# Five full expert tiles taken ahead of the last batch's routing, in both MoE layers of a four-layer hybrid kernel

## The chip, the cores and the metric

The kernel runs on one core of one Trainium2 chip. The metric is device time in microseconds (us) for the whole program, median of three runs. Engines are named as in the profile: PE is TensorE, DVE is VectorE, ACT is ScalarE, POOL is GpSimd, SP is SyncE, which here only starts transfers.

## What is computed

Four residual layers over x of shape 4 x 256 x 256 (1024 tokens, in eight tiles of 128): attention A, MoE, attention B, MoE, each on a layernorm of x. All in float32.

```
x = x + attn_a(layernorm(x))     # 16 heads; rotary parts; causal
x = x + ffn(layernorm(x))
x = x + attn_b(layernorm(x))     # 32 heads of 8, 8 KV heads; causal
x = x + ffn(layernorm(x))        # the same weights as the first ffn

def ffn(x):                      # E = 8 experts, I = 688, top 2
    logits = xf @ router_w.T
    top_vals, top_idx = top_k(logits, 2)
    top_w = softmax(top_vals)
    combine = sum(one_hot(top_idx, E) * top_w[..., None], axis=1)
    for e in range(E):
        h = silu(xf @ Wg[e].T) * (xf @ Wu[e].T)
        out = out + combine[:, e:e+1] * (h @ Wd[e].T)
```

## The kernel before

Layers are numbered 0 (attention A), 1 (MoE), 2 (attention B), 3 (MoE). Every engine has its own program, written out in order at the end of the file; semaphores tie them together.

**Attention** goes batch by batch (4 batches, b = 0 to 3), in groups of four heads: 4 groups in layer 0, 8 in layer 2. For a group, PE makes scores, then shifted scores (`shifted_tensor`), ACT their exponentials, PE the product with V (`pv_tensor`, L515 and L519), DVE copies it out (`pv_vector`), PE transposes it (`out_t_tensor`, L532), DVE divides (`divide_vector`). After the last group of a batch: `all_t_tensor` (L542), `out_scalar`, `project_tensor` (L555), `add_vector`.

**Routing** of batch b-1 is woven into attention of batch b: layernorm (`norm_tensor`, L351), logits (L1093), the two largest (`largest_vector`), then `rank_tensor` (L1104), which counts with bf16 matmuls how many earlier tokens chose the same expert, and `slots_vector` (ends at L1136), which turns ranks into addresses. POOL then writes the tokens into a table `slots_in` in HBM, ordered by expert (four indirect transfers L1207), and their numbers into `row_of_slot` (four more, L1210). The last batch has nothing to be woven into: `route_last_*` does it after attention, and `tiles_vector` (L1144 to L1161) then makes the list of expert tiles.

**Expert tiles.** 2048 routed rows over 8 experts need at most 23 tiles of 128 rows. For each: SP loads the rows (L1219), PE transposes them (L1252), `tile_up` makes gate and up products (L1265, 16 matmul records in the trace), ACT the SiLU, DVE the product (L1326), PE transposes the hidden rows (`tile_hidden`, L1276), DVE and ACT copy them, `tile_down` (L1287, 12 records) multiplies by the down weights, ACT copies out and POOL scatters the result (L1241) and loads the next tile's row numbers (L1232, L1233). PE reads the tile's expert number from the list with a register load (`expert_of`, L1256). The loop is software-pipelined: hidden(i-1), transpose(i+1), up(i), down(i-1).

**Where the weights lie.** All gate/up weights live in `wgu` (eight experts of 1376 KB), all down weights in `R1` (5504 KB). Attention A uses the same room before: queries and keys of even batches (0, 2) lie in `R1`, those of odd batches (1, 3) in the places of experts 5 to 7 of `wgu`; smaller buffers lie in experts 3 and 4. So SP loads experts 0 to 2 early, the down weights after batch 2's last shifted scores (in two transfers, L1500 and L1501), then experts 3, 5, 6, 7, 4, of which 5 to 7 wait for batch 3's last shifted scores. In layer 2 the last batch's queries and keys lie in `R2`, where the expert tiles keep their rows too.

Of the kernel before, what the change touches and what calls it, by code (L numbers as in the profile page):

```python
# [17 lines left out]
P = 128  # L18
# [26 lines left out]

SLOTS = E * T + (SLOTS_T - ROUTED // P) * P
# [4 lines left out]
def shape_constants():  # L51

    def bf16(x):
# [24 lines left out]
        np.arange(24, dtype=np.float32) * P,  # L78
    ]).astype(np.float32)
# [8 lines left out]
def build_hybrid(nc, dr, out):  # L88

    ctx = ExitStack()  # L90
    with ctx:
# [29 lines left out]
        def room(o, n):  # L121
            return wgu[:, o:o + n]

        ODD = 5 * KD * GU
        stacks = [(R1[0:RA, 0:HA * S], R1[0:RA, HA * S:2 * HA * S]),
                  (room(ODD, HA * S)[0:RA, :], room(ODD + HA * S, HA * S)[0:RA, :])]
# [11 lines left out]
        assert o <= ODD  # L138
# [44 lines left out]
        small = wb[:, o:o + 200]; o += 200  # L183
# [15 lines left out]
        o = 0  # L199
        cmp = XN[:, 1024 + o:1024 + o + 72].rearrange("p (e j) -> p e j", j=E); o += 72  # L200
        ntl = XN[:, 1024 + o:1024 + o + E]; o += E
        base = XN[:, 1024 + o:1024 + o + E + 1]; o += E + 1
        ecm = XN[0:1, 1024 + o:1024 + o + 24 * E].rearrange("p (i e) -> p i e", e=E); o += 24 * E
        ecb = XN[0:1, 1024 + o:1024 + o + 24 * E].rearrange("p (i e) -> p i e", e=E); o += 24 * E
        eidf = XN[0:1, 1024 + o:1024 + o + 24]; o += 24
        first = XN[0:1, 1024 + o:1024 + o + 24]; o += 24
        rowf = XN[0:1, 1024 + o:1024 + o + 24]; o += 24
        eid = XN[0:1, 1024 + o:1024 + o + 24].bitcast(I32); o += 24
        row = XN[0:1, 1024 + o:1024 + o + 24].bitcast(I32); o += 24
        rows = XN[:, 1024 + o:1024 + o + 2].bitcast(I32); o += 2  # L210
        assert o <= 1024
# [16 lines left out]
        xn_b = R2[:, 5632:6144].rearrange("p (t d) -> p t d", t=2)  # L228

# [80 lines left out]
        def normed_rows(l, b):  # L310


            if l in (0, 2):
                return xn[:, 2 * b:2 * b + 2, :]
            return xn[:, 0:2, :] if b == B - 1 else xn_a if l == 1 else xn_b
# [4 lines left out]
        def normed_vector(l, b):  # L320
# [4 lines left out]
            if l in FF:  # L325
                later(v, s["transposed"], b)
                if 0 < b < B - 1:
                    v.wait_ge(FF[l][f"scatter{(b - 1) % 2}"], 64 * ((b - 1) // 2 + 1))
# [216 lines left out]

        def project_tensor(l, b):
# [6 lines left out]
            for t in range(2):  # L553
                for kk in range(KD):
                    last = nc.tensor.matmul(BK[6][:, t * D:(t + 1) * D], oT[:, kk, t * P:(t + 1) * P], wo[:, kk, :],  # L555
# [3 lines left out]
        def add_vector(l, b):  # L559
# [3 lines left out]
            nc.vector.tensor_tensor(xb, xb, BK[6][:, :].rearrange("p (q d) -> p q d", q=2), ALU.add).then_inc(s["added"], 1)  # L563
# [69 lines left out]
        def attend_a_tensor(b):  # L633
            max_tensor(0, b)
            nc.tensor.wait_ge(AT[0]["max_e"], b + 1)
            for g in range(GA):
# [7 lines left out]
                if g >= 1:  # L644
                    pv_tensor(0, b, g - 1)
                if g == 1 and b > 0:
                    logits_tensor(1, b - 1)
                if g == 2 and b > 0:
                    nc.tensor.wait_ge(FF[1]["copied"], b)
# [4 lines left out]
        def end_a_tensor(b, step):  # L654
            if step == 0:
                pv_tensor(0, b, GA - 1)
                if b > 0:
                    nc.tensor.wait_ge(AT[0]["divided"], b * GA + GA - 2)
                    rank_tensor(1, b - 1)
            if step == 1:  # L660
                if b > 0:
                    nc.tensor.wait_ge(FF[1]["slot"], b)
# [4 lines left out]
        def end_a_vector(b, step):  # L667
            if step == 0:
                pv_vector(0, b, GA - 1)
                if b > 0:  # L670
                    slots_vector(1, b - 1)
# [14 lines left out]
        def attend_a_vector(b):  # L686
            for g in range(GA - 1):
                pv_vector(0, b, g)
                if g == 0 and b > 0:
                    logits_vector(1, b - 1)  # L690
                if g >= 1:
                    divide_vector(0, b, g - 1)
                if g == 2 and b > 0:
                    largest_vector(1, b - 1)
# [24 lines left out]
        def attend_b_tensor():  # L719
# [3 lines left out]
            for n in range(RUN + 3):  # L723
# [6 lines left out]
                if g >= 5 and b > 0:  # L730
                    nc.tensor.wait_ge(AT[2]["divided"], n - 2)
                if g == 5 and b > 0:
                    norm_tensor(3, b - 1)
                if g == 6 and b > 0:
# [972 lines left out]
```

## Time and profile before

| what | value |
|---|---|
| median of 3 runs | 941.76 us (940.12 to 944.01) |
| the profiled execution | 940.44 us, span 938.5 us |
| PE busy | 793.6 us, 85% of the span |
| DVE, ACT, POOL busy | 358.8, 246.9, 223.5 us |
| L1265, up products, PE | 223.2 us |
| L1287, down products, PE | 127.0 us |

The span is the first to the last instruction of the program. The page's row of granted clock is in tenths of full speed; PE is granted either full speed (2.4 GHz) or half (1.2 GHz), and a slice with 7 in it holds both. PE's row of busy tenths (40 equal slices) falls to 6 and 4 in slices 12 and 13 and to 8 and 2 in slices 30 and 31: these are the two places between an attention and its MoE, and the places of the change. The 7, 3, 3, 7 of slices 21 to 24 is the end of the first MoE and the start of attention B, which the change doesn't touch.

### The profile page before, as it was taken

How to read it: one execution, taken by the hardware profiler on the slowest of the kernel's cores; microseconds unless marked ns; L12 is line 12 of the kernel's file. 1: busy time of each engine (PE TensorE's matmuls, PEld its weight loads, DVE VectorE, ACT ScalarE, POOL GpSimd, SP SyncE). 2: the span in 40 equal slices, each digit the busy share in tenths (PEclk: the TensorE clock that was granted, in tenths of full speed). 3: DMA queues.
4: the chain of work that ended last, by engine and by line, in shares of the span. 5: the costliest groups of instructions: out<-in, count | busy, mean ns of one | idle time of the engine just before them, and what ended most of it. 6: DMA issues, size and time to landing. Idle time of an engine off the chain costs nothing.

```text
span 938.5 us, 14815 instructions
## 1 busy us (share of the span) xinstructions
PE 793.6 (85%) x5008; PEld 605.5 (65%) x5009; DVE 358.8 (38%) x860; ACT 246.9 (26%) x493; POOL 223.5 (24%) x260
## 2 busy tenths in 40 slices
PE   1989899999964999999973379999982999999990
PEld 1767677777743777777752347777762777777770
DVE  8444253653432212212235576576443222222112
ACT  1102104123322222222213204545451222222221
POOL 8441022340233112221123400012324111222212
PEclk9999899999985999999995779999995999999995
DMA  6963904125953061000203451120402001110004
GB/s 186 404 145 123 321 27 113 35 58 118 272 218 113 29 218 48 34 32 25 66 23 90 130 142 33 41 61 31 155 24 67 21 31 34 34 34 34 28 18 140
DMA packets 47472, 88.09 MB, mean 94 GB/s; under 512 B 8667, under 2 KB 36699, under 8 KB 45307
## 3 DMA queue, kind: packets, MB, share of 16 engines
q1 hardware_dynamic: 35887, 54.49, 20.7%
q0 software_dynamic: 7568, 30.97, 9.1%
q10 hardware_dynamic: 3968, 1.97, 0.8%
q8 instruction: 32, 0.52, 0.2%
q14 instruction: 17, 0.14, 0.1%
HBM read 52.27 MB, written 35.13 MB: 93 GB/s over the span
## 4 chain that ended last, share of the span: by engine, by line
PE 80%; DVE 8%; DMA 5%; issue 2%; ACT 1%; POOL 1%; SPq 1%; ACTq 0%; POOLq 0%; DVEq 0%
PE bank L1265 23%; PE bank L1287 13%; PE bank L860 8%; PE bank L486 4%; PE bank L441 4%; PE bank L1276 3%; PE bank L497 3%; PE bank L515 3%; PE bank L431 2%; PE bank L484 2%; PE bank L555 2%; PE bank L532 2%; DMA PTR<-rows_out 2%; DVE stat L308 2%; PE bank L1252 1%
## 5 line engine op out<-in xcount | busy, mean ns | idle before, releaser
L1265 PE MATMUL bank<-wgu,R 128*128 x736 | 223.2, 457 | 0.0
L1265 PEld LDWEIGHTS bank<-wgu,R 128*128 128x128 f32 x736 | 138.1, 193 | 64.9 <-issue 2.1
L1287 PE MATMUL bank<-R 112*128 (+1 forms) x552 | 127.0, 379 | 1.3 <-DVE R L1329 1.3
L1326 DVE TENSOR_TENSOR R<-R,bank 128x344 f32<-128x344 f32 x92 | 47.2, 513 | 194.7 <-PE bank L1265 194.7
L1287 PEld LDWEIGHTS bank<-R 112*128 112x128 f32 (+1 forms) x552 | 104.7, 190 | 22.6 <-issue 1.8
L625 ACT ACTIVATE PTR<-bank 128x512 f32<-128x512 f32 x144 | 83.5, 597 | 86.8 <-PE bank L486 71.5
L1241 POOL DMA_INDIRECT rows_out<-R,XN x46 | 46.5, 1011 | 177.4 <-ACT R L1317 162.8
L1329 DVE COPY R<-bank 112x512 f32<-112x512 f32 x46 | 31.8, 691 | 112.4 <-PE bank L1276 112.4
L1303 ACT ACTIVATE R<-bank 128x344 f32<-128x344 f32 x92 | 42.0, 457 | 118.7 <-PE bank L1265 118.7
L574 DVE TENSOR_REDUCE XN<-bank 128x2 f32<-128x512 f32 x96 | 63.1, 684 | 9.3 <-PE bank L441 9.3
L1317 ACT ACTIVATE R<-bank 128x256 f32<-128x256 f32 x46 | 17.7, 384 | 152.6 <-PE bank L1287 152.6
L1233 POOL DMA_DIRECT2D XN<-row_of_slot x46 | 25.7, 558 | 133.4 <-issue 130.8
L570 DVE TENSOR_REDUCE XN<-bank 128x4 f32<-128x512 f32 x48 | 33.1, 689 | 45.6 <-PE bank L431 45.0
L484 PE MATMUL bank<-XN,sel_sb 96*128 96x256 bf16 x192 | 49.7, 276 | 0.0
L595 DVE COPY XN<-bank 128x256 f32<-128x256 f32 x48 | 20.2, 420 | 76.2 <-PE bank L519 75.9
L903 POOL TENSOR_TENSOR R<-wgu 128x256 f32<-128x256 f32 x32 | 23.2, 724 | 108.0 <-DVE wgu L875 102.8
L351 PE MATMUL bank<-ident_sb,XN 128*128 128x128 f32 x40 | 9.3, 381 | 45.9 <-DVE XN L331 45.9
L1207 POOL DMA_INDIRECT slots_in<-R,stat x12 | 11.6, 970 | 144.6 <-DVE stat L1136 141.9
L860 PE MATMUL bank<-xnT,R 128*128 128x256 f32 (+2 forms) x176 | 41.5, 392 | 2.3 <-DVE wgu L875 1.5
L860 PE MATMUL bank<-wgu,R 96*128 96x256 f32 (+1 forms) x176 | 40.7, 384 | 0.8 <-issue 0.8
L860 PEld LDWEIGHTS bank<-xnT,R 128*128 128x128 f32 (+2 forms) x176 | 31.9, 186 | 11.1 <-issue 5.1
L1276 PE MATMUL bank<-ident_sb,R 128*112 128x128 f32 (+1 forms) x276 | 37.8, 273 | 1.4 <-DVE R L1326 1.4
(159 smaller groups left out, 1250.8 us busy)
## 6 DMA issues: line engine op xcount, KB each, us to landing
wgu<-in_wgu SPq DMA_DIRECT2D x10, 1376.0 KB, 9.8
slots_in<-PTR POOLq DMA_DIRECT2D x1, 9088.0 KB, 26.7
row_of_slot<-in_unused POOLq DMA_DIRECT2D x2, 4544.0 KB, 17.3
R<-slots_in SPq DMA_DIRECT2D x46, 128.0 KB, 2.0
R<-R SPq DMA_DIRECT2D x32, 128.0 KB, 2.4
wgu<-R SPq DMA_DIRECT2D x32, 128.0 KB, 2.4
PTR<-rows_out SPq DMA_DIRECT2D x16, 256.0 KB, 3.2
R<-in_wd SPq DMA_DIRECT2D x1, 3584.0 KB, 17.3
```

The lines of the kernel that those rows point to most:

```text
L441: last = nc.tensor.matmul(bank[1 + i][:, j * S:(j + 1) * S], q(h)[:, P:S], k(h)[:, :], start=False, stop=j == 1, skip_group_check=True)
L484: nc.tensor.matmul(bank[i][:, j * S:(j + 1) * S], sel[:, h:h + 1].broadcast_to([PARTS * 32, P]), nT[:, :], start=False, stop=False, skip_g ...
L486: last = nc.tensor.matmul(bank[i][:, j * S:(j + 1) * S], k(h)[:, 0:P], q(h)[:, :], start=False, stop=j == 1, skip_group_check=True)
L574: nc.vector.tensor_reduce(nmax[:, 1, 4 * g + 2 * i:4 * g + 2 * i + 2], bank[1 + i][:, :].rearrange("p (n s) -> p n s", n=2), AX, ALU.max, ...
L625: nc.scalar.activation(PT[:, g % 2, i, :], banks(l, g, True)[i][:, :], ACT.Exp, scale=scale).then_inc(s["exps"], 1)
L860: last = nc.tensor.matmul(dst, w, r, start=kk in (0, None), stop=kk in (1, None))
L1241: g.indirect_dma_start(y_d[:, :], bass.IndirectOffsetOnAxis(ap=rows[:, p:p + 1], axis=0), yo[:, p, :], None).then_inc(s[f"ys{p}"], 16)
L1265: last = nc.tensor.matmul(BK[2 * half + gu][:, 0:IH], xsT[:, p, kk, :], wgu[:, bass.ds(e * (KD * GU) + (kk * GU + gu * I + half * IH), IH) ...
L1276: last = nc.tensor.transpose(BK[4 + c // 4][0:CH[c], (c % 4) * P:(c % 4 + 1) * P], hh[:, CO[c]:CO[c] + CH[c]], ident[:, :])
L1287: last = nc.tensor.matmul(BK[7][:, 0:D], hT[0:CH[c], p, c, :], wd[0:CH[c], bass.ds(e * (6 * D) + c * D, D)], start=c == 0, stop=c == 5)
L1303: a.activation(sg[:, half * IH:(half + 1) * IH], BK[2 * half][:, 0:IH], ACT.Silu).then_inc(s["silu"], 1)
L1326: v.tensor_tensor(hh[:, half * IH:(half + 1) * IH], sg[:, half * IH:(half + 1) * IH], BK[2 * half + 1][:, 0:IH], ALU.mult).then_inc(s["hid ...
```

## The change

Batches 0 to 2 send 1536 rows to 8 experts. However they fall, at least `FULL_T` = 5 tiles of 128 rows are full by then. The changed kernel lists five such tiles once batch 2 is routed, and runs them while batch 3 is routed; the other 18 tiles come from a second list (`REST_T`). The number of tiles stays 23.

- `tiles_vector` is called twice: by `full_tiles_vector` (17 short DVE instructions, during attention of the last batch) and for the rest (15, after the last batch's slots).
- `finish_tensor`, `finish_vector`, `finish_scalar` replace `route_last_*` and the first steps of `experts_*`: an order written out by hand that weaves the last batch's transposes, projection, layernorm, logits and rank into tiles 0 to 3.
- In attention, logits and rank of the batch before come one step earlier, and rank is moved from the end of a batch (layer 0) or group 7 (layer 2) into the groups.
- The places are exchanged: even batches' queries and keys lie in experts 5 to 7, odd ones' in `R1`. So SP loads 5, 6, 7, 3, 4 after batch 2, and the down weights are loaded after batch 3's last shifted scores, on POOL's queue (`load_down_gpsimd`).
- Batch 2's normed rows of layer 1 get a buffer of their own (`xn_c`). Down products of tiles 0 to 3 go to bank 5, since bank 7 serves the routing.

```diff
+BEFORE = (B - 1) * S * TOPK
+FULL_T = (BEFORE - E * (P - 1) + P - 1) // P
+REST_T = SLOTS_T - FULL_T
@@ attend_a_vector
-                pv_vector(0, b, g)
                 if g == 0 and b > 0:
                     logits_vector(1, b - 1)
+                    largest_vector(1, b - 1)
+                if g == 1 and b > 0:
+                    slots_vector(1, b - 1)
+                pv_vector(0, b, g)
+                if g == 1 and b == B - 1:
+                    full_tiles_vector(1)
@@ finish_tensor(l)
+            out_t_tensor(a, b, heads(a)[0] - 1)
+            nc.tensor.wait_ge(FF[l]["eid"], 1)
+            nc.tensor.wait_ge(s_wgu, 16 * (E if l == 1 else E + 2))
+            e = [expert_of(i) for i in range(FULL_T)]
+            tile_transpose(l, 0, 0, 0)
+            tile_transpose(l, 1, 0, 1)
+            tile_up(l, 0, 0, 0, e[0], [0])
+            all_t_tensor(a, b)
+            tile_up(l, 0, 0, 0, e[0], [1])
+            project_tensor(a, b)
+            hidden_and_next(0, 0, 0)
+            tile_up(l, 1, 0, 1, e[1])
+            norm_tensor(l, b)
+            nc.tensor.wait_ge(s_wd, 32)
+            tile_down(l, 0, 0, 0, e[0])
+            logits_tensor(l, b)
+            hidden_and_next(1, 0, 1)
+            tile_up(l, 2, 1, 0, e[2], [0])
+            rank_tensor(l, b)
+            tile_up(l, 2, 1, 0, e[2], [1])
+            tile_down(l, 1, 0, 1, e[1])
...
+            tile_down(l, 3, 1, 1, e[3])
+            nc.tensor.wait_ge(FF[l]["eid"], 2)
+            tile_transpose(l, 5, 2, 1)
+            nc.tensor.wait_ge(FF[l]["y_e"], FULL_T - 1)
@@ experts_gpsimd(l)
+            tile_gpsimd(l, 0, 0, 0)
+            tile_gpsimd(l, 1, 0, 1)
+            scatter_gpsimd(l, B - 1)
+            tile_gpsimd(l, 2, 1, 0)
+        def load_down_gpsimd():
+            nc.gpsimd.wait_ge(AT[0]["shifted"], B * 3 * GA)
...
+            nc.gpsimd.dma_start(wdv[0:CH[0], :, 0:4 * D], dr["wd4"].rearrange("e p m -> p e m")).then_inc(s_wd, 16)
+            nc.gpsimd.dma_start(wdv[0:CH[5], :, 4 * D:6 * D], dr["wd2"].rearrange("e p m -> p e m")).then_inc(s_wd, 16)
@@ experts_sync(l), before the first rows are loaded
+            if l == 3:
+                nc.sync.wait_ge(AT[2]["shifted"], B * 3 * GB)
```

The order on PE at the end of attention A, before the change. L1104 is rank, L532 the transposes of single groups, L542, L555, L351 and L1093 the last batch's, L1256 the register load, L1252 the first tiles' transposes.

```order
L519 MATMUL bank<-PTR,vaug 32x128 x4
L1104 MATMUL bank<-wb 128x8 x11
L532 MATMUL bank<-ident_sb,XN 128x128 x4
L542 MATMUL bank<-ident_sb,XN 128x128 x4
L555 MATMUL bank<-R,XN 128x256 x4
L351 MATMUL bank<-ident_sb,XN 128x128 x4
L1093 MATMUL bank<-wb,xnT 128x8 x4
L1104 MATMUL bank<-wb 128x8 x23
L1256 TENSOR_LOAD XN
L1256 ISA x2
L1252 MATMUL bank<-ident_sb,R 128x128 x4
```

The same place after it, from the same product with V (now L537). L1364 are tile transposes, L1377 up products, L560 is all_t, L576 the projection, L1390 hidden transposes, L369 the layernorm's.

```order
L537 MATMUL bank<-PTR,vaug 32x128 x4
L550 MATMUL bank<-ident_sb,XN 128x128 x4
L1368 TENSOR_LOAD XN
L1368 ISA x2
L1364 MATMUL bank<-ident_sb,R 128x128 x4
L1377 MATMUL bank<-wgu,R 128x344
L560 MATMUL bank<-ident_sb,XN 128x128 x4
L576 MATMUL bank<-R,XN 128x256 x4
L1390 MATMUL bank<-ident_sb,R 112x128 x4
L369 MATMUL bank<-ident_sb,XN 128x128 x4
L1404 MATMUL bank<-R 128x256
L1113 MATMUL bank<-wb,xnT 128x8 x4
```

Rows that only repeat are left out here: the register load stands five times, the up product eight times for tile 0 (four on each side of all_t) and eight for tile 1 between L1390 and L369. Two tiles' worth of up products now stand between the last product with V and the last batch's layernorm.

POOL's order in layer 1, after the change. L1319 and L1322 are the scatters of a batch, L1589 and L1590 the down weights, L1345 loads row numbers, L1353 scatters a tile's result.

```order
L1319 DMA slots_in<-R,stat 9088x256 x4
L1322 DMA row_of_slot<-wb,stat 9088x128 x4
L1589 DMA R<-in_wd 112x8x1024
L1590 DMA R<-in_wd 120x8x512
L1344 TENSOR_LOAD XN
L1345 DMA XN<-row_of_slot 128x1
L1353 DMA rows_out<-R,XN 11136x256
L1319 DMA slots_in<-XN,stat 9088x256 x4
```

Before, batch 3's scatter followed batch 2's at once, and no weights were on this queue. Now the down weights stand behind batch 2's eight scatters, and batch 3's scatter (`slots_in<-XN`) behind the results of tiles 0 and 1 (left out: the second row load and the second tile's rows, which repeat).

## Rows read from the trace of the kernel before

**Rows 1.** Page, part 4: shares of the chain that ended last.
```profile
PE 80%; DVE 8%; DMA 5%; issue 2%; ACT 1%; POOL 1%; SPq 1%; ACTq 0%; POOLq 0%; DVEq 0%
```
**Rows 2.** PE's longest wait from 260 to 310 us: in total, times, longest.
```profile
PE bank L1252 <- DMA R<-slots_in: 9.9, 1, 9.9
```
**Rows 3.** PE's timeline around layer 1: start, us, what, idle time before it.
```profile
242.13 0.60 PE L542 MATMUL bank<-ident_sb,XN 128*128 128x128 f32 x4
243.42 1.99 PE L555 MATMUL bank<-R,XN 128*128 128x256 f32 x8 [0.69 <-ACT XN L630]
...
266.81 0.64 PE L515 MATMUL bank<-PTR,vaug 128*32 128x256 f32 x8 [0.27 <-DVE XN L595]
...
268.60 0.42 PE L1104 MATMUL bank<-wb 128*128 128x8 bf16 x11 [0.93 <-DVE wb L1125]
...
281.34 1.08 PE L351 MATMUL bank<-ident_sb,XN 128*128 128x128 f32 x4 [3.54 <-DVE XN L331]
...
297.42 0.66 PE L1252 MATMUL bank<-ident_sb,R 128*128 128x128 f32 x2 [9.85 <-DMA R<-slots_in]
...
299.09 5.95 PE L1265 MATMUL bank<-wgu,R 128*128 x16
...
313.87 0.82 PE L1276 MATMUL bank<-ident_sb,R 128*112 128x128 f32 x6
...
314.75 4.79 PE L1265 MATMUL bank<-wgu,R 128*128 x16
319.38 2.76 PE L1287 MATMUL bank<-R 112*128 x12
...
338.17 0.82 PE L1276 MATMUL bank<-ident_sb,R 128*112 128x128 f32 x6
```
**Rows 4.** PE's timeline around layer 3, same columns.
```profile
699.50 0.41 PE L532 MATMUL bank<-ident_sb,XN 128*128 128x128 f32 x2 [0.65 <-DVE XN L605]
...
723.31 0.66 PE L1252 MATMUL bank<-ident_sb,R 128*128 128x128 f32 x2 [9.77 <-DMA R<-slots_in]
...
764.44 0.82 PE L1276 MATMUL bank<-ident_sb,R 128*112 128x128 f32 x6
```
**Rows 5.** Stretches: engines' busy us and counts, granted clock, DMA share, GB/s.
```profile
270.00:275.00 5.00, 2.97 (x10) 1.87 (x11) 1.00 (x4) 1.46 (x2) 3.87 (x4) 0.57 1.01 419
...
300.00:305.00 5.00, 5.00 (x15) 2.79 (x14) 0.51 (x1) 1.94 (x3) 1.15 (x2) 0.86 0.10 27
```
**Rows 6.** Line L1256 from 270 to 340 us: duration ns min/median/max, first and last start.
```profile
L1256 PEldq FUSED_REGOPS  x14: 46/151/165, 292.2 to 335.5; - x14
L1256 PEldq TENSOR_LOAD <-XN x11: 298/302/483, 291.7 to 335.1; - x11
```
**Rows 7.** DVE's timeline, first and last instruction of the tile list in layer 1.
```profile
288.33 0.22 DVE L1144 TENSOR_TENSOR XN<-bank,wb 128x64 f32<-128x64 f32 x1
...
291.49 0.17 DVE L1161 CAST XN<-XN 1x24 int32<-1x24 f32 x1
```
**Rows 8.** POOL's timeline: batch 2's scatters, first and last; a tile's result and row load.
```profile
270.15 0.97 POOL L1207 DMA_INDIRECT slots_in<-wgu,stat  x1 [26.37 <-DVE stat L1136]
...
279.06 0.96 POOL L1210 DMA_INDIRECT row_of_slot<-wb,stat  x1 [0.30 <-issue]
...
741.54 1.01 POOL L1241 DMA_INDIRECT rows_out<-R,XN  x1 [11.35 <-ACT R L1317]
745.15 0.55 POOL L1233 DMA_DIRECT2D XN<-row_of_slot  x1 [2.61 <-issue]
```
**Rows 9.** DMA issues in layer 1: count, KB each, us from issue to landing.
```profile
R<-in_wd SPq DMA_DIRECT2D x1, 3584.0 KB, 17.3
R<-in_wd SPq DMA_DIRECT2D x1, 1920.0 KB, 28.2
...
slots_in<-XN,stat POOLq DMA_INDIRECT x1, 2.4
...
R<-slots_in SPq DMA_DIRECT2D x1, 128.0 KB, 2.1
```

More of the change, by code:

```diff
@@ L197, in build_hybrid, with passed @@
         assert o <= KD * (D + 2 * KVB * HDB), o
[L199 to L211, printed above, removed]
+        o = 1536
+        cmp = XN[0:1, o:o + 72].rearrange("p (e j) -> p e j", j=E); o += 72
+        ntl = XN[0:1, o:o + E]; o += E
+        base = XN[0:1, o:o + E + 1]; o += E + 1
+        jump = XN[0:1, o:o + E + 1]; o += E + 1
+        left = XN[0:1, o:o + E]; o += E
+        over = XN[0:1, o:o + E]; o += E
+        total = XN[0:1, o:o + E]; o += E
+        assert o <= 1664
+        o = 1672
+        eid = XN[0:1, o:o + 24].bitcast(I32); o += 24
+        row = XN[0:1, o:o + 24].bitcast(I32); o += 24
+        rows = XN[:, o:o + 2].bitcast(I32); o += 2
+        taken = XN[0:1, o:o + E]; o += E
+        eidf = XN[0:1, o:o + 24]; o += 24
+        rowf = XN[0:1, o:o + 24]; o += 24
+        def passed(n, at):
+            return [XN[0:1, at + k * n * (E + 1):at + (k + 1) * n * (E + 1)].rearrange("p (i e) -> p i e", e=E + 1)
+                    for k in range(2)]
+        early_lists, late_lists = passed(FULL_T, o), passed(REST_T, 1024)
+        assert o + 2 * FULL_T * (E + 1) <= 1896 and 1024 + 2 * REST_T * (E + 1) <= 1536
         FILLS = 8
@@ L722, in attend_b_tensor @@
             max_tensor(2, 0)
-            for n in range(RUN + 3):
+            for n in range(RUN + 1):
                 b, g = n // GB, n % GB
@@ L762, in attend_b_vector @@
             parts_vector(2, 0)
-            for n in range(RUN + 3):
+            for n in range(RUN + 1):
                 b, g = n // GB, n % GB
@@ new lines, in tiles_vector @@
+            if not first:
+                link(v.tensor_tensor(left, ntl, taken, ALU.subtract),
+                     v.tensor_tensor(jump[:, 0:E], jump[:, 0:E], taken, ALU.add))
+            link(v.tensor_tensor(cmp, (ntl if first else left)[:, None, :].broadcast_to([1, E + 1, E]),
+                                 small[0:1, 80:152].rearrange("p (e j) -> p e j", j=E), ALU.mult))
+            link(v.tensor_reduce(base, cmp, AX, ALU.add))
+            link(v.tensor_tensor(ecm, small[0:1, 152:152 + n, None].broadcast_to([1, n, E + 1]),
+                                 base[:, None, :].broadcast_to([1, n, E + 1]), ALU.is_ge))
@@ L1274, in tile_hidden @@
             later(nc.tensor, s["hte_s"], i)
-            for c in range(6):
+            for c in chunks:
+                if c == 4 and isinstance(i, int):
+                    later(nc.tensor, s["y_e"], i)
                 last = nc.tensor.transpose(BK[4 + c // 4][0:CH[c], (c % 4) * P:(c % 4 + 1) * P],
@@ L1555, in _ @@
             project_b_gpsimd()
-            for b in range(B):
+            for b in range(B - 1):
                 scatter_gpsimd(3, b)
@@ L1578, in _ @@
                 attend_a_vector(b)
-            for step in range(3):
+            for step in range(2):
                 end_a_vector(B - 1, step)
-            add_vector(0, B - 1)
-            route_last_vector(1)
+            finish_vector(1)
             experts_vector(1)
@@ L1643, in _ @@
                 attend_a_tensor(b)
-            for step in range(3):
+            for step in range(2):
                 end_a_tensor(B - 1, step)
-            all_t_tensor(0, B - 1)
-            project_tensor(0, B - 1)
-            route_last_tensor(1)
+            finish_tensor(1)
             experts_tensor(1)
```

333 lines of the change are left out of this document (194 added, 139 removed).

## The prediction, made before the changed kernel ran

> **What bounds the kernel now.** Read the shares of the last chain first: PE holds 80% of it, DMA 5% [rows 1]. So the kernel is bound by PE's work, and time can only be won where PE stands still. PE's waits next: in the stretch from 260 to 310 us it stood 9.9 us for the first expert rows [rows 2], and 3.54 us for the last batch's layernorm [rows 3]. The timeline then gives the whole hole. The last product with V starts at 266.81 and the first tile's transposes at 297.42, and only the last batch's short steps lie between [rows 3]. In layer 3 the same hole runs from the last group's transpose at 699.50 to 723.31 [rows 4]. Last, the granted clock: 0.57 in the stretch from 270 us, 0.86 in that from 300 us [rows 5], so PE fell to half speed in the hole and came back only after the first up products had run for a while (5.95 us against 4.79 us for the same sixteen later, 1.2 us lost) [rows 3]. Once it runs, PE has no gaps: a tile takes 8.10 us, from (338.17 - 313.87) / 3 [rows 3].
>
> I follow one mark through before and after, the start of the hidden transposes of tile 4: 338.17 in layer 1 and 764.44 in layer 3 [rows 3, 4]. Behind that mark the same 18 tiles follow, PE-bound in both kernels. The time won is how much earlier the mark comes, once for each layer.
>
> **1. The attention loops.** Logits and rank change places with products with V; the matmuls stay, but for six more small ones in the rank of batch 2. In group 2 PE now waits for the slots (five dependent DVE instructions, at the 0.25 us of those of the tile list [rows 7] some 1.2 us) behind one product with V (0.64 us and a shorter one [rows 3]), in place of a similar wait at the end of a batch. I cost batches 1 and 2 at nothing, 1 us either way. For the last batch in layer 1 the rank (0.42 us before [rows 3], 0.5 with its six more) and 0.6 us of that wait now lie ahead of the last product with V: it starts at 267.9 instead of 266.81 [rows 3]. It ends at 268.7. A group's transposes cost 0.41 us and 0.65 of wait for the division before them [rows 4]; of the two groups left, one wait is covered: 1.1 to 1.5 us, 269.8.
>
> The first tile list is 17 DVE instructions. The 13 of the old list took 3.3 us (288.33 to 291.66) [rows 7], so about 3.8 us. In layer 1 a group's float32 scores and product on PE hide them. In layer 3 a group's scores are bf16 and short, and the next copy of a product with V stands behind the list on DVE: PE waits between 0 and the whole 3.8 us, and I take 2, as about half of it finds cover in one group. The last transpose comes at 701.3 instead of 699.50 [rows 4].
>
> **2. Up to the first tile.** PE needs five expert numbers. One load is 0.30 us, with register work of 0.15 us behind it, the first 0.48 us [rows 6]: 2.6 us, and with the small gaps between them I take 3.1. Nothing else can run on PE meanwhile. The rows themselves are there in time: batch 2's scatter starts about 262.3 instead of 270.15 [rows 8], its fourth write lands 3.8 + 2.4 us later and the load of the rows takes 2.1 [rows 9], some 270.8. So the first tile's transposes start at 269.8 + 3.1 = 272.9 in layer 1 (before: 297.42 [rows 3]) and 701.3 + 3.1 = 704.4 in layer 3 (before: 723.31 [rows 4]).
>
> **3. From there to the wait for the down weights.** Transposes and up products of tile 0 at a half-speed start, as before: 299.09 + 5.95 - 297.42 = 7.6 us. Inserted: all_t 0.6 and projection 2.0 (at full speed [rows 3]). Hidden transposes and the next tile's: 314.75 - 313.87 = 0.9. Up products of tile 1: 319.38 - 314.75 = 4.6. Layernorm's transposes 0.5 (1.08 at half speed [rows 3]). Sum 16.2: PE is at the wait at 289.1 in layer 1 and at 720.6 in layer 3. ACT's table loads for square root and SiLU, and the layernorm on DVE, fit under these.
>
> **4. The down weights.** They are now asked for after batch 3's last shifted scores, and POOL first has to issue eight scatters of batch 2. Those took from 270.15 to 280.02, 9.9 us [rows 8]; from 262.3 they end at 272.2, and the weights are issued at about 272.8. How long the load takes is the largest unknown. Before, the pair took 28.2 us from issue to landing of the second [rows 9], with one batch's scatters (0.75 MB) among it, which I take off as 2 us: 26. The low bound is what all transfers together reached when gate/up weights were loaded, 419 GB/s [rows 5]: 5504 KB in 13.5 us. I take 26, since it is this same transfer with the same shapes: it lands at 298.8. PE stands for 9.7 us, falls to half speed again and loses another 1.2 us when it starts. In layer 3 the weights are there, and this term is nothing.
>
> The Trainium skill, page "DMA: Bandwidth & Descriptors", section "Anatomy of one DMA", gives 2.0 us plus the bytes at 436 GB/s for a transfer from GpSimd's queue; by it the pair would take about 15 us and land at 288, and PE would not wait. The row of before (17.3 us for the first alone) speaks against it. The same page, section "Latency and other measured facts", tells of copies that fall to about half the rate when rows lie a large power of two apart; that would keep this load slow on any queue, and no run here shows it yet.
>
> **5. From the wait to the mark.** Down 0, three steps of 8.10, logits 1.0, rank 0.4, tile 5's transposes and a short wait for a bank 0.5, less the transposes that step 3 doesn't have 0.2: 2.6 + 24.3 + 1.7 = 28.6 us. Layer 1: 298.8 + 28.6 + 1.2 = 328.6, that is 9.6 us earlier than 338.17. Layer 3: 720.6 + 28.6 = 749.2, 15.2 us earlier than 764.44.
>
> **6. The last batch's rows.** They are needed for tile 5. POOL scatters tiles 0 and 1 first: from the end of down 1 there are 0.8 us to POOL's start, 4.2 us for the result and the next row load (741.54 to 745.70 [rows 8]), then three scatter steps of 1.27, 2.4 to land, 0.8 for SP, 2.1 to load [rows 8, 9]: 14.2 us. PE needs 16.0 us from there to the transposes of tile 5. Hidden, with 1.8 us in hand; if that cover goes, each us over it is paid twice, once for each layer.
>
> **Sum.** 9.6 + 15.2 = 24.8 us. The profiled execution took 940.44 us, 1.3 under the median, so 915.6 against it; I predict 916.0.
>
> **Rivals.**
> A. The down weights come fast (any time from 14 to 17 us). Then PE doesn't wait in layer 1 and keeps its clock: 9.7 + 1.2 more, 905. For it: gate/up weights of a similar size did run at 419 GB/s [rows 5], and fewer other transfers run now. Against: 17.3 and 28.2 us for the same bytes [rows 9]. Anything between gives 905 to 916.
> B. Rows come late. The loads of tiles 2 and 3 run while the down weights fill all engines, and tile 5's rows hang on a chain with 1.8 us in hand. If POOL's writes land in 6 us instead of 2.4, PE waits 2 us twice; if tile 2's rows wait for the whole load, up 1 and the layernorm (5 us) come after it instead of under it. 919 to 926.
> C. The clock stays low. Between the tiles PE now does short steps with waits. If it ran at half speed from the first transposes to the mark, 45 us of work would take 90, in both layers 90 us more, against 25 won: about 1005, slower. It decides from about 25 us of extra time, that is if over a quarter of the stretch is at half speed. Against it: in the rows of before, full speed came back within 3 us of the first up products (1.2 us lost [rows 3]).
> D. The first tiles don't come early at all, because PE also waits for all eight gate/up weights and the list. The five loads begin where the down weights did, a whole batch of groups ahead. They are 6880 KB against 5504, so even at the slow rate of [rows 9] they take 35 us (28.2 x 1.25), and the first tile starts later than that. If they came only with the rest, all would be as before, 940.
>
> **How the numbers follow.** The forecast (911 to 919): 0.50. A and what lies between: 0.27. B: 0.17. C: 0.02. D and small gains: 0.04. The range of 903 to 924 holds A, the forecast and most of B. A measurement of this kernel can tell 0.5% (4.7 us) from no change. Faster by over that 0.96, within 0.02, slower 0.02.
>
> **What would show it.** In the profile after: PE's longest wait in layer 1 is that of the first down products for `R<-in_wd`, near 10 us (A: under 1). Time from issue to landing of the two: near 26 us. The first tile's transposes at about 273 and 704. Granted clock of 1.0 from there but for that wait. No wait of over 1 us at tile 5's transposes; if there is one, B. Hidden transposes of tile 4 at 329 and, in layer 3, 15 us earlier relative to the last product with V than the old one. The prediction is wrong if PE waits for anything else for over 3 us between the marks, or if batches 1 and 2 cost more than 1 us each in either attention.

## The result: 931.4 us, 11 us faster where 25 were forecast

The changed kernel took 931.37 us (median of 4 runs, 930.45 to 933.83) against 942.38 us for the kernel before: ratio 0.9895, 95% interval 0.9871 to 0.9919. The sign was right and the size was not: the time lies above the range of 903 to 924. The profiled execution has a span of 928.7 us, 9.8 under that of before; the ratio gives 9.9 us. A label such as x2 names a run of the section on the experiments.

The page's part 4 of the changed kernel (shares of the chain that ended last) answers to [rows 1]:

```profile
PE 74%; DMA 8%; DVE 8%; issue 6%; POOL 2%; ACT 1%; SPq 0%; ACTq 0%; POOLq 0%; DVEq 0%
```

DMA went from 5% to 8% because the load of the down weights, 27.32 us, now lies on the chain. The rise of "issue" from 2% to 6% is for the most part no stall of PE. The chain in order of time (start, us, what) shows where it lies; its 4.95 us have their like before the change (4.47):

```profile
103.59 4.95 issue
...
233.64 28.39 issue
...
332.34 2.12 issue
...
752.23 2.10 issue
```

From the weights the chain goes back to POOL, which issued them behind batch 2's scatters and had stood idle for 28.6 us before the first of these, until the slots came at 262.26. PE worked in that stretch, so a good part of its fall from 80% to 74% is this detour too. Only the two pieces of 2.1 us are new stalls of PE's sequencer on this chain. PE's timeline around layer 1 (start, us, what, idle time before it) answers to [rows 3]:

```profile
269.79 0.41 PE L550 MATMUL bank<-ident_sb,XN 128*128 128x128 f32 x2 [0.72 <-DVE XN L627]
...
273.54 0.69 PE L1364 MATMUL bank<-ident_sb,R 128*128 128x128 f32 x2 [3.34 <-issue]
...
300.48 5.28 PE L1404 MATMUL bank<-R 112*128 x12 [10.82 <-DMA R<-in_wd]
...
312.60 2.76 PE L1404 MATMUL bank<-R 112*128 x12
...
331.75 0.39 PE L1364 MATMUL bank<-ident_sb,R 128*128 128x128 f32 x2
334.46 0.84 PE L1390 MATMUL bank<-ident_sb,R 128*112 128x128 f32 x6 [2.33 <-issue]
```

The first tile starts 24 us earlier than at 297.42 [rows 3]. Then PE stands 10.8 us for the down weights, runs tile 0's down product in 5.28 us instead of 2.76, and stands 2.3 us more right at the mark, which comes at 334.46: 3.7 us earlier than 338.17 [rows 3], where 9.6 were forecast. The same in layer 3, beside [rows 4]:

```profile
706.92 0.69 PE L1364 MATMUL bank<-ident_sb,R 128*128 128x128 f32 x2 [3.16 <-DMA R<-slots_in]
...
722.84 2.76 PE L1404 MATMUL bank<-R 112*128 x12
...
754.32 0.84 PE L1390 MATMUL bank<-ident_sb,R 128*112 128x128 f32 x6 [2.31 <-issue]
```

That mark is 10.1 us earlier than 764.44 [rows 4], so layer 3 itself gave 6.4 where 15.2 were forecast. The weights' landing (DMA issues, KB each, us from issue to landing) stands beside [rows 9], and the stretches (engines' busy us and counts, granted clock, DMA share, GB/s) beside [rows 5]:

```profile
R<-in_wd POOLq DMA_DIRECT2D x1, 3584.0 KB, 18.5
R<-in_wd POOLq DMA_DIRECT2D x1, 1920.0 KB, 27.3
```

```profile
285.00:290.00 5.00, 4.66 (x19) 2.97 (x17) 3.08 (x10) 3.95 (x7) 0.00 (x0) 1.00 1.04 236
290.00:295.00 5.00, 0.00 (x0) 0.00 (x0) 0.00 (x0) 0.29 (x1) 0.00 (x0) 0.68 0.98 215
295.00:300.00 5.00, 0.00 (x0) 0.00 (x0) 0.00 (x0) 0.00 (x0) 0.00 (x0) 0.50 0.75 147
300.00:305.00 5.00, 4.52 (x11) 3.63 (x12) 0.00 (x0) 0.00 (x0) 0.00 (x0) 0.50 0.01 3
```

In the wait the granted clock falls to 0.50, that is 1.2 GHz, and it stays there through tile 0's down product.

Last, attention B, where the forecast put nothing for batches 1 and 2. PE's waits from 585 to 672 us (in total, times, longest), first of the kernel before, then of the changed one:

```profile
PE bank L532 <- DVE wb L1111: 1.2, 2, 0.6
PE bank L532 <- DVE stat L1136: 0.9, 2, 0.5
```

```profile
PE bank L369 <- DVE R L349: 2.9, 2, 1.5
PE bank L550 <- DVE stat L1159: 2.5, 2, 1.3
PE bank L550 <- DVE wb L1132: 1.2, 2, 0.6
```

L369 is the layernorm's transposes, L349 the division in it, L1159 the write of the slots. Two waits of 1.45 us are new and the two for the slots grew by 0.8 each: 4.5 us. By PE's timeline, from the max_t transposes of batch 1 (two transposes of row maxima, once for each batch) to those of batch 3 it is 75.40 us before (592.48 to 667.88) and 80.03 after (589.59 to 669.62).

### The profile page after: what moved, and what is told of

It is laid out like the page before. It is cut to its first block, busy times and chain, and to the rows that moved or that the text cites. A ratio compares the mean times of both kernels' runs of the same rounds, so it can differ in the third digit from the quotient of the medians.

```text
span 928.7 us, 14805 instructions
## 1 busy us (share of the span) xinstructions
PE 793.1 (85%) x5020; PEld 603.6 (65%) x5021; DVE 365.0 (39%) x902; ACT 290.4 (31%) x527; POOL 225.2 (24%) x262
## 4 chain that ended last, share of the span: by engine, by line
PE 74%; DMA 8%; DVE 8%; issue 6%; POOL 2%; ACT 1%; SPq 0%; ACTq 0%; POOLq 0%; DVEq 0%
PE bank L1377 22%; PE bank L1404 13%; PE bank L880 9%; PE bank L1390 3%; PE bank L459 3%; PE bank L504 3%; DMA R<-in_wd 3%; PE bank L515 2%; PE bank L449 2%; PE bank L533 2%; PE bank L502 2%; DVE XN L596 2%; DMA PTR<-rows_out 2%; DVE stat L324 2%; PE bank L550 1%
## 5 line engine op out<-in xcount | busy, mean ns | idle before, releaser
L1377 PE MATMUL bank<-wgu,R 128*128 x736 | 224.6, 458 | 0.0
L1377 PEld LDWEIGHTS bank<-wgu,R 128*128 128x128 f32 x736 | 137.7, 193 | 64.7 <-issue 2.4
L1404 PE MATMUL bank<-R 112*128 (+1 forms) x552 | 129.5, 385 | 12.1 <-DMA R<-in_wd 10.8
L1353 POOL DMA_INDIRECT rows_out<-R,XN x46 | 45.5, 989 | 191.0 <-ACT R L1434 179.8
L1319 POOL DMA_INDIRECT slots_in<-R,stat x16 | 15.5, 971 | 176.9 <-DVE stat L1159 173.2
L1345 POOL DMA_DIRECT2D XN<-row_of_slot x46 | 26.1, 567 | 129.7 <-issue 127.1
L1390 PE MATMUL bank<-ident_sb,R 128*112 128x128 f32 (+1 forms) x276 | 40.5, 274 | 5.1 <-issue 4.6
L369 PE MATMUL bank<-ident_sb,XN 128*128 128x128 f32 x40 | 8.5, 357 | 38.5 <-DVE XN L349 38.5
L1390 PEld LDWEIGHTS bank<-ident_sb,R 128*112 128x112 f32 (+1 forms) x276 | 32.3, 135 | 12.2 <-issue 5.7
```

What stands on the lines that cost most here:

```text
L1353: g.indirect_dma_start(y_d[:, :], bass.IndirectOffsetOnAxis(ap=rows[:, p:p + 1], axis=0), yo[:, p, :], None).then_inc(s[f"ys{p}"], 16)
L1377: last = nc.tensor.matmul(BK[2 * half + gu][:, 0:IH], xsT[:, p, kk, :], wgu[:, bass.ds(e * (KD * GU) + (kk * GU + gu * I + half * IH), IH) ...
L1390: last = nc.tensor.transpose(BK[4 + c // 4][0:CH[c], (c % 4) * P:(c % 4 + 1) * P], hh[:, CO[c]:CO[c] + CH[c]], ident[:, :])
L1404: last = nc.tensor.matmul(down_bank(i)[:, 0:D], hT[0:CH[c], p, c, :], wd[0:CH[c], bass.ds(e * (6 * D) + c * D, D)], start=c == 0, stop=c == 5)
```

## The experiments

All ratios are against the kernel before, run on the same chip. The marks are those that the prediction follows, the start of tile 4's hidden transposes in layers 1 and 3: 334.46 and 754.32 in the changed kernel.

**Attention B's order, undone (x1).** For batches 1 and 2 the steps of the batch before go back one group later, on PE, DVE and ACT; the last batch keeps the new order.

```
-                if 4 <= g <= 6 and b > 0:
+                k = g if b == B - 1 else g - 1
+                if 4 <= k <= 6 and b > 0:
...
-                if g == 4 and b > 0:
+                if g == (4 if b == B - 1 else 5) and b > 0:
```

> The changed kernel with one part undone: in attention B, for batches 1 and 2, layernorm, logits and rank of the batch before stand again in groups 5, 6 and 7 (and DVE's statistics behind the maxima), as in the kernel before; batch 3 keeps the early order. Theory 'order in attention B': in the trace of the changed kernel PE waits 1.45 us twice for the normed rows and about 1 us twice more for the slots, and the stretch from the first scores of batch 1 to the projection of batch 2 is 4.6 us longer than before; undone, it is 4.6 us shorter, and the whole run about 4.6 us below the changed kernel (926.8 against 931.4). Rival 'exchange of places': the loss comes from where queries, keys and weights lie or from other transfers; then this run is as the changed kernel, within 1 us.

Measured: 930.0 us (926.64 to 934.54), ratio 0.9869, 0.9824 to 0.9913. In the trace the stretch between the max_t transposes is 75.39 us, 4.64 shorter; the waits at L369 are gone and those for the slots are back at 0.9 us. The total alone could not tell this from no change. The span is only 1.1 us under the changed kernel's, since this execution lost 2.4 us between layer 1's mark and batch 1's max_t, where the edit changes nothing: 1.6 of them in the first step behind the mark, with a granted clock of 0.66 from 335 to 340 us (1.00 in the changed kernel). x8 below settles it.

**PE's wait for y(3) moved, tiles 5 and 6 taken out of the loop (x2).** y(3) is tile 3's result, which ACT copies out of its bank; `y_e` counts these copies.

```
             tile_transpose(l, 5, 2, 1)
-            nc.tensor.wait_ge(FF[l]["y_e"], FULL_T - 1)
...
-                if c == 4 and isinstance(i, int):
+                if c == 4 and isinstance(i, int) and i < FULL_T:
...
-            with nc.tensor.Fori(2, (SLOTS_T - 3) // 2) as r:
+            step(5, 2, 1)
+            step(6, 3, 0)
+            with nc.tensor.Fori(3, (SLOTS_T - 3) // 2) as r:
```

> The changed kernel with PE's wait for the result of tile 3 taken from before the loop and put before the two hidden chunks that need it (tiles 5 and 6 written out, so that the wait can stand there); the last two tiles lose their needless waits for the same. Theory 'register loads': the 2.3 us in which PE stands before the hidden transposes of tile 4 are two loads of expert numbers that PE can only begin once the wait ahead of the loop is over; moved, they run while down 3 does, and the mark (hidden transposes of tile 4) comes 2.0 to 2.3 us earlier in each layer; with the waits inside the last tiles some 5 us in all: 926.5. Rival 'ACT': the wait is really for ACT, which does the exponential with its table load and the copy of tile 3 there; then the mark moves by under 0.5 us and the run stays at 931.

Measured: 925.41 us (923.07 to 925.92), ratio 0.9808, 0.978 to 0.9836. At the mark PE's timeline of this kernel reads:

```profile
333.77 0.84 PE L1389 MATMUL bank<-ident_sb,R 128*112 128x128 f32 x6 [0.16 <-issue]
```

2.33 us of "issue" are down to 0.16. From down 0 to the mark it is 31.4 us in layer 1 (changed kernel: 34.0, of which 0.6 is down 0's own slower run) and 29.0 in layer 3 (changed kernel: 31.5). In the changed kernel the wait for y(3) was met at 332.33, when ACT had copied it out. But it held PE's sequencer, so the loop's register loads behind it, which need nothing of y(3), started only then: the first at 332.6, the second at 333.5, and their register work ends at 334.2. x2 took the loop's start away from there together with the wait, so the share of the loop's start in these 2.1 us is not told apart. In the last tiles, where a like wait is gone too, each layer is 0.8 us shorter.

**Why the down weights are slow: the size of the pieces (x3).** Both tensors stored so that each partition's data is one run of 32 KB or 16 KB, in HBM and in SBUF, instead of eight of 4 and 2 KB.

```
-            nc.gpsimd.dma_start(wdv[0:CH[0], :, 0:4 * D], dr["wd4"].rearrange("e p m -> p e m")).then_inc(s_wd, 16)
+            nc.gpsimd.dma_start(R1[0:CH[0], 0:E * 4 * D], dr["wd4"]).then_inc(s_wd, 16)
...
-        "wd4": down[:, 0:CO[4]].reshape(E, 4, CH[0], D).transpose(0, 2, 1, 3).reshape(E, CH[0], 4 * D),
+        "wd4": down[:, 0:CO[4]].reshape(E, 4, CH[0], D).transpose(2, 0, 1, 3).reshape(CH[0], E * 4 * D),
```

> The changed kernel with the down weights laid out by partition in HBM and in SBUF: one run of 32 KB and one of 16 KB for each partition, in place of pieces of 4 and 2 KB (the host only orders them). Same bytes, same queue, same moment. Theory 'layout': the 27.3 us to landing come from the pieces and their pitch; with whole rows the pair goes at the 420 GB/s of the gate/up weights and lands in 14 to 16 us; PE's wait of 10.8 us and its half-speed start are gone, about 12 us: 919. Rival 'this moment': the rate is set by what else goes on then, and landing stays above 24 us; the run stays within 2 us of 931.

Measured: 932.2 us (931.43 to 932.97), landing 18.2 and 28.3 us: the same rate. The pieces do not set it. They may set something else. PE waited for a tile's rows, which were loaded beside the weights, once for 10.6 us, where it did not wait in the changed kernel:

```profile
295.12 0.69 PE L1364 MATMUL bank<-ident_sb,R 128*128 128x128 f32 x2 [10.60 <-DMA R<-slots_in]
```

It then found the weights in place (down 0 at 303.18), so two waits changed places. That long pieces hold up what is loaded beside them fits this; no other run has them.

**The queue (x4).** The same two loads from ACT's queue, issued at 265.17 and 265.61 us instead of 272.15 and 273.03.

```
-            nc.gpsimd.dma_start(wdv[0:CH[0], :, 0:4 * D], dr["wd4"].rearrange("e p m -> p e m")).then_inc(s_wd, 16)
+            nc.scalar.dma_start(wdv[0:CH[0], :, 0:4 * D], dr["wd4"].rearrange("e p m -> p e m")).then_inc(s_wd, 16)
```

> The changed kernel with the two transfers of down weights issued from ACT's queue, as soon as batch 3's last shifted scores are done (about 267) instead of from POOL's behind eight scatters (272.2). Theory 'rate is the transfer's own': 26 to 28 us to landing as before, but begun 5 us earlier: PE's wait shrinks from 10.8 to 5 or 6 us, the run is 5 us below the changed kernel, 926. Rival 'POOL's queue is slow for it': landing falls to under 20 us and the wait is gone, 919. Other rival: first tiles' rows (SP's queue) come late behind it, and the first tile's transposes move from 273.5 to over 276.

Measured: 927.09 us (925.14 to 929.02), ratio 0.9838. Landing:

```profile
R<-in_wd ACTq DMA_DIRECT2D x1, 3584.0 KB, 18.1
R<-in_wd ACTq DMA_DIRECT2D x1, 1920.0 KB, 28.4
```

The rate is the same from another queue. In the changed kernel the eight scatters of batch 2 stand ahead of the load, here five of them are issued during it, and the landing differs by 1.1 us; so neither the scatters nor POOL makes it slow. PE's wait for weights went, and 12.0 us of waits for tile rows (9.8 and 2.2) came in layer 1. The 15.2 us that the expectation of x11 names are those of the whole run, with 3.2 us in layer 3 that the changed kernel has too. The mark in layer 1 is at 328.24, 6.2 us earlier than in the changed kernel. 1.4 of it is attention that ended earlier in this execution. The other 4.8 are gained: the five register loads (3.3 us) now lie under the wait for rows, and down 0, with no wait before it, takes 2.76 us instead of 5.28.

**The spacing of the rows in HBM (x5).** Each row is padded, from 4096 to 5504 bytes in the first tensor and from 2048 to 2752 in the second; the pieces and the place in SBUF stay. (The expectation calls the 4096 and 5504 values; they are bytes, and its 11008 is wrong.)

```
-        "wd4": down[:, 0:CO[4]].reshape(E, 4, CH[0], D).transpose(0, 2, 1, 3).reshape(E, CH[0], 4 * D),
+        "wd4": np.pad(down[:, 0:CO[4]].reshape(E, 4, CH[0], D).transpose(0, 2, 1, 3).reshape(E, CH[0], 4 * D), ((0, 0), (0, 0), (0, 352))),
```

> The edit pads each row of the down weights in HBM from 4096 to 5504 values (and from 2048 to 2752 values in the second tensor... in bytes 11008 and 5504 for each expert's row), so that rows no longer lie a power of two apart; pieces, bytes, queue and place in SBUF stay. Theory A (the spacing of the rows in HBM makes the load slow; the Trainium skill, page 'DMA: Bandwidth & Descriptors', section 'Latency and other measured facts', tells of half the rate for power-of-two spacing): the two loads land some 9 and 14 us after issue instead of 18.5 and 27.3, PE's wait of 10.8 us for them falls below 1, the clock isn't lowered a second time, and the time is about 931 - 11 - 2 = 918. Rival B (the loads are slow for another reason, such as that they fill 112 and 120 of 128 partitions, or that the eight scatters and the row loads stand between them): landing 18 and 27 us as before, time 931.

Measured: 931.89 us (930.92 to 932.37), landing 19.4 and 27.7 us. Nothing moved, so the spacing does not set this rate. It says nothing against the Trainium skill, page "DMA: Bandwidth & Descriptors", section "Latency and other measured facts": its row is on large powers of two, with the loss at 2 MiB and more and the full rate still at 512 KiB, while the rows here lie 4 and 2 KB apart. The prediction and the expectation were wrong to apply it to this load.

**The count of partitions (x6).** The weights padded with rows of zeros, so that each load fills 128 partitions; the spacing as in the changed kernel.

```
-            nc.gpsimd.dma_start(wdv[0:CH[0], :, 0:4 * D], dr["wd4"].rearrange("e p m -> p e m")).then_inc(s_wd, 16)
+            nc.gpsimd.dma_start(wdv[:, :, 0:4 * D], dr["wd4"].rearrange("e p m -> p e m")).then_inc(s_wd, 16)
```

> The edit pads the down weights with rows of zeros so that both loads fill 128 partitions in place of 112 and 120 (6144 KB instead of 5504); the spacing of the rows in HBM stays at a power of two. Theory B (the count of partitions makes the load slow, because the rows are then spread unevenly over the 16 engines): landing near 9 and 15 us, PE's wait of 10.8 us gone, about 919. Theory A (the spacing does): 12% more bytes at the same rate, landing at 20.5 and 30.5 us, PE waits some 3 us longer, about 934.

Measured: 926.48 us (922.93 to 930.02), ratio 0.9857. Twelve per cent more bytes land 7.8 us sooner:

```profile
R<-in_wd POOLq DMA_DIRECT2D x1, 4096.0 KB, 14.7
R<-in_wd POOLq DMA_DIRECT2D x1, 2048.0 KB, 19.5
```

PE's wait fell from 10.8 to 2.1 us; 7.8 us of that is the faster load, the rest is PE, which came to the wait 0.9 us later after the issue than in the changed kernel. By the total, x6 and the changed kernel cannot be told apart (the intervals of the ratios, 0.9825 to 0.9889 and 0.9871 to 0.9919, overlap); x9 does that. The DMA view from 285 to 290 us, in the middle of the load, shows what differs (packets, MB, share of 16 engines), first of the changed kernel, then of this one:

```profile
DMA packets 353, 1.18 MB, mean 236 GB/s; under 512 B 57, under 2 KB 67, under 8 KB 353
## 3 DMA queue, kind: packets, MB, share of 16 engines
q0 software_dynamic: 339, 1.17, 101.4%
```

```profile
DMA packets 509, 1.94 MB, mean 388 GB/s; under 512 B 26, under 2 KB 39, under 8 KB 509
## 3 DMA queue, kind: packets, MB, share of 16 engines
q0 software_dynamic: 486, 1.93, 101.7%
```

All 16 engines are busy in both. With 112 or 120 partitions a packet takes longer on average: 16 x 5 us over 339 packets is 0.24 us each, against 0.165 with 128. So the load was not short of requests. What holds the packets up, no view shows.

**How the rate goes with partitions (x10).** The changed kernel with its loads cut by partitions, 96 and 16, then 64 and 56.

```
+            for lo, hi in ((0, 96), (96, CH[0])):
+                nc.gpsimd.dma_start(wdv[lo:hi, :, 0:4 * D], dr["wd4"].rearrange("e p m -> p e m")[lo:hi, :, :]).then_inc(s_wd, 16)
+            for lo, hi in ((0, 64), (64, CH[5])):
+                nc.gpsimd.dma_start(wdv[lo:hi, :, 4 * D:6 * D], dr["wd2"].rearrange("e p m -> p e m")[lo:hi, :, :]).then_inc(s_wd, 16)
```

> One look at how the rate goes with the partitions. The changed kernel, with its two down loads cut in four by partitions and nothing else changed: 96 and then 16 partitions of the first, 64 and then 56 of the second. From one landing to the next: by the Trainium skill, page 'SBUF - State Buffer', section 'Door 1: The DMA port swizzle', partitions 0 to 63 reach 8 of 16 ports, so the load on 64 (1024 KB) should take 4.8 us at 218 GB/s, that on 56 (partitions 64 to 119, 896 KB) as long, and that on 16 (512 KB) far longer than a sixth of the one on 96 (3072 KB). Theory B1 (each port's load decides): 96 partitions, with 8 on each even port, and 4 on each odd port, take as long as all 128 would, 9.6 us. Rival B2 (what decides is whether the pieces of one engine fall on one port, as they do with 128 partitions and do not with 112 or 120): the piece of 64 runs no faster than that of 56. PE's wait stays or grows, the time is 931 to 938.

Measured (a single run, so no reading rests on its total): 940.29 us, and

```profile
R<-in_wd POOLq DMA_DIRECT2D x1, 3072.0 KB, 19.1
R<-in_wd POOLq DMA_DIRECT2D x1, 1024.0 KB, 27.0
R<-in_wd POOLq DMA_DIRECT2D x1, 896.0 KB, 31.0
...
R<-in_wd POOLq DMA_DIRECT2D x1, 512.0 KB, 22.3
```

The order of issue is 96, 16, 64, 56 partitions, at 274.59, 275.42, 275.96 and 276.66 us. From one landing to the next: 16 partitions 22.3 + 0.83 - 19.1 = 4.0 us (130 GB/s), 64 partitions 5.2 us (200 GB/s), 56 partitions 4.7 us (195 GB/s). These are rough, since one load can begin before the one ahead has landed. In the same way the second load has 203 GB/s with 120 partitions (changed kernel) and 366 with 128 (x6). And 3072 KB on 96 partitions took 4.4 us longer than 4096 KB on 128. The Trainium skill, page "SBUF — State Buffer", section "Door 1: The DMA port swizzle (why `[64,N]` ≈ `[32,N]`)", makes the rate depend on how many of 16 ports a range of partitions reaches, with 0 to 63 on eight of them. The 200 and 195 GB/s for 64 and for 56, which reach eight ports each, agree with it (it has 196 for 0 to 63). But by its table 96, 112 and 120 partitions, which reach all ports and put no more than eight partitions on any, should cost no more than 128, and here they do: theory B1 falls. Rival B2, that with 128 partitions each engine keeps to a port and with other counts they cross, is contradicted by none of these numbers, but it gives no figure for any of them either. No view here shows a packet's port, so it stays open; shown is that full 128 is the fast case.

**All the mending together (x7).** Padding, 128 partitions, attention B's order undone, the waits of x2, and this:

```
-            e = [expert_of(i) for i in range(FULL_T)]
+            e = [expert_of(0)]
...
             tile_up(l, 0, 0, 0, e[0], [0])
+            e += [expert_of(i) for i in range(1, FULL_T)]
```

> All the mending together: padded rows and 128 partitions for the down weights, the order of attention B undone for batches 1 and 2, the wait for y(3) moved behind tiles 5 and 6 which leave the loop, no chunk wait in the last tiles, and expert numbers 1 to 4 loaded behind the first half of tile 0's up products. Terms from the traces so far: 5.9 us for waits and registers (925.4 against 931.4), 4.6 for the order of attention B, 1 to 2 for the later loads of expert numbers, and 10.8 + 1.4 if either theory on the down weights holds. About 908 then, and about 920 if neither does.

Measured: 909.59 us (908.93 to 911.21), ratio 0.9673, 0.9658 to 0.9688. The marks are at 323.07 and 734.62, 15.1 and 29.8 us earlier than before. PE's timeline:

```profile
271.40 0.43 PE L1372 MATMUL bank<-ident_sb,R 128*128 128x128 f32 x2 [0.67 <-DMA R<-slots_in]
...
292.27 4.60 PE L1412 MATMUL bank<-R 112*128 x12 [5.27 <-DMA R<-in_wd]
```

The 3.34 us of loads ahead of the first tile are gone in layer 1. In layer 3 the distance from the last transpose to the first tile fell only from 3.57 to 2.16 us, since PE then waits there for the tile's rows. Of the wait for the weights 5.3 us are left.

**One part of x7 left out at a time: the order of attention B (x8).**

> x7_all_mended with attention B's loops left as the change has them. Theory (the order costs 4.64 us in attention B, between max_t of batch 1 and of batch 3: 80.03 us in the changed kernel, 75.39 with the order undone): 80.0 between the two, and 909.6 + 4.6 = 914.2. Rival (the 4.6 us are given back later, as the run of x1_order_b could not tell): 910 to 911.

Measured: 915.78 us (914.41 to 918.6), ratio 0.973, 0.9708 to 0.9752; 80.02 us between the max_t transposes against 75.37 in x7. The order costs 0.0057 of 941.8 = 5.4 us, with intervals that do not overlap, and 4.65 of it is that stretch. It is not given back.

**The down weights on 112 and 120 partitions again (x9).** This undoes the padding of the rows as well, which by x5 makes no difference.

> x7_all_mended with the down weights loaded on 112 and 120 partitions again, from rows of the old spacing. Theory (the count of partitions sets the rate): landing at 18.5 and 27.3 us in place of 13.8 and 18.5, PE's wait for them 5.3 + 8.8 = 14.1 us, so 909.6 + 8.8 + about 0.5 for the clock = 919. Rival (the gain of x6_all_partitions was scatter of the run, or the DMA has room elsewhere): under 913.

Measured: 920.54 us (917.94 to 921.11), ratio 0.9771, 0.9751 to 0.9792; landing 18.1 and 26.9, PE's wait 13.4 us. The partitions are worth 0.0098 x 941.8 = 9.2 us, from one wait in one layer (8.1) and the clock behind it (tile 0's down product takes 5.48 us instead of 4.60).

**The down weights asked for earlier (x11).** The scatter of batch 2 takes the load between its two groups of writes.

```
-            scatter_gpsimd(1, B - 2)
-            load_down_gpsimd()
+            scatter_gpsimd(1, B - 2, load_down_gpsimd)
```

> x7_all_mended with the down weights issued between the four writes of rows and the four writes of the rows' numbers of batch 2, that is at about 268 instead of 272.7. Theory (PE's wait of 5.3 us is the load's end alone): landing at 286.5 instead of 291.2, wait about 1.5 with the rows later by 1 to 2, time 906. Rival (the rows of tiles 0 to 2 queue behind the load on the same engines, as in x4_down_act_queue, where PE waited 15.2 us for rows): PE waits more than 4 us for R<-slots_in and the time is 909 or more.

Measured: 909.59 us (908.91 to 911.59), ratio 0.9667, 0.9648 to 0.9686: no gain. The rival held. The wait for weights went, and in its place PE waited for the rows, from 262 to 300 us:

```profile
PE bank L1373 <- DMA R<-slots_in: 6.8, 2, 5.7
```

## Why the prediction was wrong, by its own steps

The sign and most of the path were right; the price was not, because one term was put at nothing and one was left out. It fell short by 15.0 us of span (9.8 instead of 24.8): 5.9 to the mark in layer 1 and 8.8 from there to the mark in layer 3; behind it nothing was lost but 0.3.

**Step 1 failed in attention B**: "batches 1 and 2 at nothing, 1 us either way". It cost 4.6 us (x1, x8), 2.3 for each batch, which is also one of the prediction's own signs of being wrong. The step priced the move by what stands on PE and took the wait for the slots for one that only changes its place. In attention B the groups are short, and the DVE work of the moved steps does not end in time: PE waits 1.26 us for the slots behind the one product with V, and 1.46 us for the layernorm's division (L349), twice each. That the short groups are the reason is argued from these waits; the same move cost nothing seen in attention A. In attention A the last transpose came at 269.79, as forecast (269.8). The list was right: the last batch took 2.1 us more from its projection to its last transpose (19.82 to 21.92), 1.8 forecast.

**Step 2 held within a microsecond**: 273.54 for 272.9 in layer 1; in layer 3 3.6 us from the last transpose instead of 3.1. The "issue" of 3.34 is the five loads.

**Step 3 held**: from the first transposes to the wait 289.66 - 273.54 = 16.1 us in layer 1, and 15.9 in layer 3, for 16.2.

**Step 4 held as a size, not as a reason**: landing at 300.3 for 298.8, PE's wait 10.8 for 9.7. Taking this transfer's own row and not a rate from another transfer was right, and rival A (905) stayed away. But the step took 2 us off for the scatters among it, and these are worth about 1 (27.3 us without, 28.4 with some among it, x4). It also called the rate a given. It is a choice of the layout, and 9 us could be had there (x9).

**Step 5 failed**: 28.6 us from the wait to the mark, plus 1.2 for the clock in layer 1, against 34.0 and 31.5. Three terms were short. The largest was left out: 2.3 us in each layer for `wait_ge(y_e)`, with the loop's start and the register loads queued behind it (x2). The step counted what PE computes and not what its sequencer has to get through; in the kernel before, the loads of the loop's start lay in the hole, where they cost nothing [rows 6]. The second is the clock: down 0 took 5.28 us instead of 2.76, all of it at half speed (granted clock 0.50 from 300 to 305 us), where 1.2 was taken from up products that ran partly at full speed (0.86, [rows 5]). The third is the step itself: 8.27 us a tile (315.20 to 323.47) for 8.10, where the hidden transposes are split in two, and a new wait stands ahead of their chunk 4; the last tiles of both layers have the wait too, and x2 shows 0.8 us a layer for it there.

**Step 6 held**: tile 5's transposes came at 331.75 with no wait for rows, so rival B was not the cause. C did not come either: tile 0's start, which the forecast has, and its down product in layer 1 aside, the tiles ran at full speed.

The ledger of the 15.0: order of attention B 4.6, the two stalls at `wait_ge(y_e)` 4.6, the weights' landing 1.7, the clock at down 0 1.3, longer steps 2.0 (0.6 in each layer ahead of the mark, 0.8 in the last tiles of layer 1), and 0.8 of small terms. The first two have runs of their own (x1 and x8; x2). The rest is read off the timelines by subtraction; of the longer steps x2 took away only those of the last tiles, together with the stalls, and no run isolates those ahead of the mark.

## What to carry to other kernels

When work is moved ahead of a loop, follow the sequencer as well as the engine: every semaphore wait in front of a loop also holds back the register loads behind it, and these are in the open (here 2.3 us twice); x2 put the wait behind them, where its result is first needed. Lay weights out for 128 partitions even if the last rows are zeros: 12% more bytes landed 7.8 us sooner. Don't shift work between short groups at "nothing" because the instructions are the same; look how long the group is beside the chain on the other engine.

## What the runs showed of the hardware

- In mid-load (285 to 290 us) the load on 112 and 120 partitions keeps all 16 DMA engines busy while 236 GB/s are moved; on 128 it is 388. The busy share of the engines says nothing on whether a load runs at its rate.
- Neither the size of the pieces (4 KB or 32 KB), nor the rows' spacing in HBM, nor the queue (POOL or ACT) changed that rate: the pair landed after 27.3 us in the changed kernel, 28.3 (x3), 27.7 (x5) and 28.4 (x4).
- A large load and small row loads share the engines. Both times the weights were asked for sooner, the rows came later: 12.0 us of waits for rows in place of 10.8 for weights in x4, 6.8 in place of 5.3 in x11. x11 gained nothing; x4 gained, because other losses lay under the wait.
- The clock can cost more than the wait shows: in x6 PE waited only 2.1 us, the granted clock was 1.00 in the stretch before 295 us and 0.70 in the one after it, and tile 0's down product took 4.40 us instead of 2.76. PE's timeline, then two stretches of the same kernel:

```profile
295.87 4.40 PE L1404 MATMUL bank<-R 112*128 x12 [2.13 <-DMA R<-in_wd]
```

```profile
290.00:295.00 5.00, 3.73 (x16) 2.36 (x14) 2.31 (x6) 3.33 (x6) 0.00 (x0) 1.00 0.98 372
295.00:300.00 5.00, 4.13 (x12) 3.38 (x13) 0.00 (x0) 0.00 (x0) 0.00 (x0) 0.70 0.02 7
```
